# A 256-column product in place of a 512-column one ahead of the scores in the lone cross attention

## What is computed

```python
q = (x @ Wq).reshape(B, Sq, h, d).transpose(0, 2, 1, 3)
k = (context @ Wk).reshape(B, -1, h, d).transpose(0, 2, 1, 3)
v = (context @ Wv).reshape(B, -1, h, d).transpose(0, 2, 1, 3)
scores = jnp.einsum('bhid,bhjd->bhij', q, k) * scale
attn = jax.nn.softmax(scores, axis=-1)
out = jnp.einsum('bhij,bhjd->bhid', attn, v)
...
logits = xf @ Wr + br
topv, topi = jax.lax.top_k(logits, K)
```

## Time and profile before

| | |
|---|---|
| median of 3 runs | 2300.51 us (2300.14 to 2302.67) |
| the profiled execution's own time | 2305.5 us |
| its span | 2303.7 us |
| PE busy | 2020.3 us, 88% of the span |
| DVE busy | 1730.9 us, 75% |
| ACT busy | 986.8 us, 43% |
| mean granted PE clock | 0.938 |
| the lone cross attention's steps 1 to 15 | 1948 to 2030 us after the span's start |

### The profile page before, as it was taken

How to read it: one execution, slowest core, us unless ns; L and a number is a source line. 1 busy time by engine, 2 the same in 40 slices (tenths; PEclk the granted TensorE clock), 3 DMA queues, 4 the chain that set the end, 5 groups by cost and what they waited for, 6 DMA issues and landing times.

```text
span 2303.7 us, 27778 instructions
## 1 busy us (share of the span) xinstructions
PE 2020.3 (88%) x10638; PEld 1232.6 (54%) x10638; DVE 1730.9 (75%) x2590; ACT 986.8 (43%) x1530; POOL 304.3 (13%) x338
## 2 busy tenths in 40 slices
PE   6999999999999999885658887888788889859998
PEld 4666666666666666542223443434454445636665
DVE  7777787788777789769999898989998997231111
ACT  1222222222222222238675866587658882312221
POOL 1111111111111111100000000000000000322222
PEclk9999999999999999997879887998799999869999
DMA  9000000000000100011111111011101113113442
GB/s 250 1 1 19 28 26 1 20 28 26 1 19 28 33 1 1 1 52 51 55 44 38 40 41 44 20 37 44 40 16 56 62 37 115 40 43 88 118 117 49
DMA packets 64497, 99.73 MB, mean 43 GB/s; under 512 B 12036, under 2 KB 47391, under 8 KB 64368
## 3 DMA queue, kind: packets, MB, share of 16 engines
q1 hardware_dynamic: 58416, 90.14, 12.1%
q0 software_dynamic: 5952, 7.86, 1.8%
HBM read 83.57 MB, written 15.60 MB: 43 GB/s over the span
## 4 chain that ended last, share of the span: by engine, by line
PE 55%; DVE 35%; issue 6%; ACT 3%; POOL 1%; DMA 0%; DVEq 0%; POOLq 0%; ACTq 0%
PE po L1861 9%; PE pa L1851 9%; DVE arena L1592 9%; PE pa L2444 5%; DVE arena L1582 5%; PE po L2455 4%; PE pa L2133 3%; PE pa L1788 3%; DVE arena L1600 2%; DVE arena L1159 2%; PE pt L1826 2%; DVE arena L1161 1%; PE po L1877 1%; PE pt L1773 1%; PE pa L1900 1%
## 5 line engine op out<-in xcount | busy, mean ns | idle before, releaser
L2133 PE MATMUL pa<-arena 128*128 128x512 f32 x512 | 297.2, 709 | 84.3 <-DVE arena L1600 84.3
L1592 DVE TENSOR_TENSOR_SCAN arena<-arena 128x1024 f32<-128x1024 f32 x128 | 292.4, 2284 | 16.0 <-ACT arena L929 15.9
L581 POOL TENSOR_SCALAR arena<-arena 128x2 f32<-128x2 f32 (+2 forms) x93 | 28.0, 301 | 1516.6 <-DVE arena L1440 818.6
L1861 PE MATMUL po<-arena 128*128 128x256 f32 x960 | 221.1, 382 | 0.0
L2133 PEld LDWEIGHTS pa<-arena 128*128 128x128 f32 x512 | 101.4, 217 | 215.1 <-DVE arena L1600 112.2
L1851 PE MATMUL pa<-arena 128*128 128x512 f32 x480 | 212.2, 594 | 1.9
L1233 DVE TENSOR_TENSOR arena<-pa,arena 128x512 f32<-128x512 f32 x256 | 158.6, 682 | 63.6 <-PE pa L1788 63.5
L913 ACT ACTIVATE arena<-arena 128x510 f32<-128x510 f32 x256 | 170.5, 717 | 52.1 <-DVE arena L1592 50.5
L1861 PEld LDWEIGHTS po<-arena 128*128 128x128 f32 x960 | 176.9, 189 | 28.0 <-issue 3.0
L736 ACT COPY arena<-po 128x512 f32<-128x512 f32 x32 | 18.8, 586 | 341.9 <-PE po L1773 341.9
L1582 DVE TENSOR_TENSOR arena<-arena 128x1024 f32<-128x1024 f32 x128 | 154.6, 1208 | 5.5 <-PE pa L2133 5.4
(11 more groups left out here) (284 smaller groups left out, 3697.0 us busy)
## 6 DMA issues: line engine op xcount, KB each, us to landing
arena<-bc_rows SPq DMA_DIRECT2D x64, 512.0 KB, 4.5
arena<-in_L_ffn_W SPq DMA_DIRECT2D x16, 1024.0 KB, 7.9
arena<-in_L_attn_W SPq DMA_DIRECT2D x8, 1024.0 KB, 6.0
arena<-rows_to_experts SPq DMA_DIRECT2D x8, 520.0 KB, 9.6
rows_to_experts<-arena SPq DMA_DIRECT2D x4, 1024.0 KB, 14.1
out<-arena SPq DMA_DIRECT2D x5, 512.0 KB
arena<-in_x SPq DMA_DIRECT2D x4, 512.0 KB, 7.2
arena<-in_rows SPq DMA_DIRECT2D x8, 256.0 KB, 3.1
```

Of the source, the lines that this page charges most:

```text
L1592: v.tensor_tensor_scan(h.rearrange(flat), decay.rearrange(flat), h.rearrange(flat), 0.0, ALU.mult, ALU.add).then_inc(scan_done, 1)
L1861: last = mm(po[s][:, ts(i, D)], gT[:, c, ts(tile, P)], w2[:, c, :], start=c == 0, stop=c == FM - 1)
L2133: last = mm(pa[c][:, :], ident, uh[i % len(uh)][:, n, :], start=g == 0 and n == 0, stop=g == NS // NG - 1 and n == NG - 1)
```

## The change

`kept_busy` gets an argument for the number of columns, and the call in `scores2`, which runs ahead of the scores of steps 1 to 15 of the lone cross attention, passes S = 256 in place of the default W = 512. No other call passes it. No instruction is added, removed or moved, on any engine: fifteen products on PE have half the moving columns and write the first half of the bank.

```diff
-        def kept_busy(bank, count):
+        def kept_busy(bank, count, cols=W):
             for _ in range(count):
-                mm(bank[:, :], ident, last_kT[:, 0, :], start=True, stop=True)
+                mm(bank[:, 0:cols], ident, last_kT[:, 0, 0:cols], start=True, stop=True)
...
                 if at.lone:
-                    kept_busy(banks[u % 2], 1)
+                    kept_busy(banks[u % 2], 1, S)
                 for b in range(2):
                     last = mm(banks[u % 2][:, b * S:(b + 1) * S], qT[ts(e, QD), 2 * j + b, ts(tile, P)],
                               keys[ts(e, QD), 2 * j + b, (tile // 2) * S:(tile // 2 + 1) * S], start=True, stop=True)
```

## The result

The changed kernel takes 2306.0 us (median of 19 runs, 2300.6 to 2317.1) against 2300.71 us before (19 runs, 2297.75 to 2305.78). The ratio is 1.0028, with a 95% interval of 1.0018 to 1.0037: slower by 5.3 us. The runs also spread more, over 16.5 us in place of 8.0, and four of the nineteen lie above 2316.

A forecast was written before the change was run, and what follows sets the result against it. PE alone was taken to bound steps 3 to 5, with its clock at half from 1970.7 to 1980.9; 2305.5 + 5.5 gave 2311.0 us, 2317.6 with another fall, and weighing the median gave 2312, range 2299 to 2321.

The forecast's parts named there:

- The direct gain: Lone cross attention: the shorter F is on the path eight times of fifteen and saves 3.1 us in all.
- The fall: Steps 1 and 2 of the lone cross attention: with short F, PE streams 0.86 us less and the clock falls to half.
- How long it lasts: Half clock from W(0) until O(0) raises it; W(0) to the end of W(3) takes 19.6 us, 7.8 us more.
- The second stretch at half, behind W(4): W(4) to the end of O(0), 13.6 us, already at half clock before; the short F takes 0.86 us off.
- the +5.5 of the sum: Lone cross attention, one further fall at the start: 7.8 - 0.9 - 1.4 = +5.5 us, so 2311.0 us.
- The offset: Whole kernel: profiled execution 5.0 us above the median, fitting a half-clock stretch not in each run; both ways lead to 2311 to 2313.
- the sum for more than one: Rival: further falls around W(8) and W(12), up to 6.6 us each; 2317.6 us and up, to 2324; chance 0.28.
- the clock doesn't care: Rival, lone cross attention: the 3.1 us or less are gained and nothing else happens, 2302.4 us; chance 0.20.
- it does better: Rival: the fall at 1970.7 doesn't come, so W(4) to O(0) takes 6.8 us less; 2296.0 us; chance 0.12.
- The skill's rule: Clock gate follows how busy PE has been; read so, steps 3 to 5 keep the clock and the change gains 3.1 us.

## Why the prediction was right, and where its sizes were off

The forecast was slower, 2312.0 us in a range of 2299 to 2321, by a fall of the clock ahead of W(0). It is 2306.0, slower, and the fall is what the runs show: short F(1) and F(2) alone cost 7.5 us, and the rest of the change alone gains 6.1. The size was less than half of the forecast, 5.3 us in place of 11.5 over the median of 2300.5.

*The direct gain.* The terms hold. F(9) and F(11) with F(13) and F(15) were put at 0.43 + 0.28 = 0.71 us a tile, and the tile is 0.64 us shorter. W(3) was to move by 0.84 us at the full clock, bound by the copy, and moves by 0.76 with the long F(1) and F(2). The wait ahead of W(8) was to grow to 1.22 us and is 1.21; that ahead of W(4) was to grow by 0.4 from 2.95 and is 3.38.

*The fall.* It came at 1950.4 us, 3.5 us ahead of W(0), and from F(2) to F(4) all ran at half, S 2.00 us, F 0.85, as written. The way to it was in part wrong. The prediction added up two short F, 0.86 us, and an idle time ahead of W(0) that grows by 0.4 us. The fall stands ahead of F(2), so only F(1) had been shortened by then, and the idle time ahead of W(0) came later and shrank to 0.19 us, since F(2) and S(2) ran at half. In all six profiles in which F(1) and F(2) have 256 columns, 64 rows or are left out there is such a fall, of 6.7 to 44.3 us. Of the six in which they are long, four have none and two have one of 3.3 us that is over by the end of the long F(2), like this one of the kernel with long F and products at all waits:

```profile
1947.40:1950.70 3.30, 3.30 (x9) 1.48 (x7) 3.20 (x5) 0.92 (x5) 0.00 (x0) 0.51 0.00 0
```

So with both long the fall is rarer and short. No run has one of them short and the other long, so what each does isn't separated.

*How long it lasts* is the step that was mis-sized. I took it that only O(0) brings the clock back, from the 10.2 us at 0.50 with PE busy, and priced W(0) to the end of W(3) at +7.8 us. (The four rows of the earlier cross attention that I took for four products, L2133 x4, are two, with two records each; in the same way W's eight records are four products.) In the profile the clock was back at 1964.0, at the end of F(4) and before any O. W(3) ended at 1968.08 + 1.10 = 1969.18, 3.7 us later than before, so the term measured +3.7. The second stretch at half, behind W(4), was one of 10.2 us in place of 13.6, so O(0) ended 1.6 us late, and not 6.9. Together these are the 5.2 us between the +5.5 of the sum and the +0.3 of the profiled run. In the kernel with short F in steps 1 and 2 only it lasted 37.4 us and ended at 1981.5, again ahead of O(0), which starts at 1983.37; without F, with the same 37.4 us, it ended with O(0). What sets the length isn't shown, and my one number for it was too firm.

*The offset.* I had the choice between the profiled execution's time and a median 5.0 us lower, and wrote that the place of a fall differs from run to run. The spread of the nineteen runs, 8.0 us before and 16.5 after, fits that. The 5.3 us are a shift of the median between two spreads. The clocks on record say more. Their median is 0.936 after the change, against 0.939 before, some 14 us more at half; the profiled pair has 0.937 and 0.938. In the two profiles the time at half differs by less, some 5 to 7 us. So the median run seems to have a further 5 to 10 us at half that the profiled one hasn't, and much of the 5.3 us is likely to lie there. The four runs above 2316 us have 0.930 or 0.931, some 30 us more at half than the profiled one. That fits two or more further falls, as in the sum for more than one (2317.6); where they lie isn't shown, as none of these runs was profiled. That the direction came out clear of the noise thus rests in part on runs that went worse than the one profiled: the sum of +5.5 us, made for the profiled execution, met +0.3 there, and that it lies next to the median's 5.3 is chance.

*The rivals.* That the clock doesn't care falls with the kernel without F and with F on 64 rows. That it does better is true of the version with long F in steps 1 and 2, 2295.65 us, where the rival had 2296.0. It had put as its condition that steps 1 and 2 hold their clock, and that version is one in which they do. Its profile still has the half clock behind W(4), but that execution took 2301.61 us, and the median clock of the twelve, 0.942 against 0.939, fits a stretch of about 14 us at half going away in most runs, which is how the rival was thought to come. Its 6.1 us are 3 more than the direct gain of about 3; that they come from the stretch behind W(4) is likely but isn't shown.

*The skill's rule.* The reading of the Trainium skill ("TensorE: Matmul & The Clock Gate", Part 1) by busy time is contradicted by 43.55 of 44.30 us busy at 0.50 with the products on 64 rows.

## What to carry to other kernels

An unread product can carry the clock of the steps behind it, and its worth isn't its own time: read the granted clock around it, and ask which wait comes next, before shortening it. The products that hold the clock should go where the engine waits anyway, and fit the wait: six ahead of W(4) alone gave 5.4 us, products at all waits gave 2.8 with the long F, whose small waits they overhang, and 6.3 and 10.2 with the short F, while shortening F alone lost 5.3. Where two of fifteen products matter most, a change to all fifteen hides a gain under a loss, and halves of the change run apart show it at once.

## What the hardware showed that I had not expected

Two 256-column halves of products that nobody waits for, in steps 1 and 2, moved 7.5 us. With too little streaming the step rate settles into a slow cycle: without F a tile takes 23.8 us in place of 17.4, with the clock at 0.50 for 20.3 us of it, PE busy 20.01 us of these, and the clock whole only for some 3.5 us behind O, from 2009.9 to 2013.5 for one. And the rows that a product works on count as well as its columns: 512 columns on 64 rows held the clock no better in steps 1 and 2 than 256 on 128, with 44.3 us at half in the profile, but in the later tiles they held it, where without any F it fell.
